# Attention and experts on one core: the first norm folded into the query weights, projections moved into the steps, token weights routed in two early parts

## The reference, cut to what matters

```python
def _layernorm(x, axis=-1, eps=1e-05):
    m = jnp.mean(x, axis=axis, keepdims=True)
    v = jnp.var(x, axis=axis, keepdims=True)
    return (x - m) / jnp.sqrt(v + eps)

# attention: q from the normed x, k and v from ctx
scores = jnp.einsum('bhqd,bhkd->bhqk', qh, kh) / scale        # scale = 8 ** -0.5
scores = jnp.where(mask, NEG_INF, scores)
attn = jax.nn.softmax(scores, axis=-1)
ctx = jnp.einsum('bhqk,bhkd->bhqd', attn, vh)                 # then @ Wo.T

# experts, on the flat normed tokens
logits = flat @ router_w.T
topk_scores, topk_idx = jax.lax.top_k(logits + router_bias, 2)
topk_scores = jax.nn.softmax(topk_scores, axis=-1)
combine = combine.at[jnp.arange(N)[:, None], topk_idx].add(topk_scores)
hidden = jax.nn.silu(gate_all) * up_all
out = jnp.einsum('nk,nkd->nd', combine, jnp.einsum('nke,ked->nkd', hidden, down_proj))
out = out + (jax.nn.silu(flat @ sh_gate.T) * (flat @ sh_up.T)) @ sh_down.T

x = x + attention(_layernorm(x), ctx, ctx, mask, ...)
x = x + experts(_layernorm(x), ...)
```

## Time and profile before

| | us |
|---|---|
| median of 3 runs | 194.75 (193.85 to 194.76) |
| the profiled execution, its own time | 194.68 |
| its span, first to last instruction | 192.9 |

### The profile page before, as it was taken

How to read it: one execution, slowest core, us unless ns; L and a number is a source line. 1 busy time by engine, 2 the same in 40 slices (tenths; PEclk the granted TensorE clock), 3 DMA queues, 4 the chain that set the end, 5 groups by cost and what they waited for, 6 DMA issues and landing times.

```text
span 192.9 us, 4173 instructions
## 1 busy us (share of the span) xinstructions
PE 179.3 (93%) x1351; PEld 131.8 (68%) x1351; DVE 168.8 (87%) x515; ACT 124.6 (65%) x280; POOL 92.1 (48%) x148
## 2 busy tenths in 40 slices
PE   7599599999999999999998799999999999999962
PEld 7497467566666666666666466778888888888841
DVE  6899999589999999989995799988899889988981
ACT  2168374777888888888885855466655665565641
POOL 5746992758988988888786690300000000000000
PEclk9969979999999999999999999999999999999997
DMA  5984910000000000000000174332363236324401
GB/s 135 286 249 92 352 40 0 5 0 0 3 2 5 0 3 0 3 0 2 5 0 3 57 198 139 110 110 82 128 180 115 72 126 171 120 82 126 120 0 54
DMA packets 13202, 15.33 MB, mean 79 GB/s; under 512 B 1665, under 2 KB 8193, under 8 KB 13057
## 3 DMA queue, kind: packets, MB, share of 16 engines
q1 hardware_dynamic: 12608, 14.57, 24.8%
q10 hardware_dynamic: 576, 0.55, 1.2%
HBM read 13.93 MB, written 1.18 MB: 78 GB/s over the span
## 4 chain that ended last, share of the span: by engine, by line
PE 61%; DVE 19%; ACT 5%; issue 5%; POOL 0%; DVEq 0%; POOLq 0%
PE bank L1013 26%; PE bank L964 12%; PE bank L945 5%; PE bank L954 5%; DVE hid L823 2%; PE bank L903 2%; ACT hid_hi L598 2%; PE bank L934 2%; DVE prob L759 2%; PE bank L924 2%; DVE smax L738 2%; DVE xn L649 2%; DVE hid_lo L815 2%; DVE cmix_sb L823 2%; PE bank L893 1%
## 5 line engine op out<-in xcount | busy, mean ns | idle before, releaser
L589 ACT ACTIVATE sig<-bank 128x512 f32<-128x512 f32 x36 | 21.5, 600 | 21.0 <-PE bank L1013 20.4
L964 PE MATMUL bank<-k_blk,q_blk 128*128 128x512 f32 x64 | 34.0, 615 | 0.0
L426 POOL TENSOR_TENSOR k_blk<-k_all,consts_sb 128x512 f32<-128x512 f32 x32 | 32.7, 1045 | 0.0
L1013 PE MATMUL bank<-xt_hi,w_hi 128*128 (+1 forms) x72 | 29.1, 405 | 0.0
L1013 PE MATMUL bank<-xt_lo,w_hi 128*128 (+1 forms) x72 | 28.4, 394 | 0.0
L1013 PE MATMUL bank<-xt_hi,w_lo 128*128 (+1 forms) x72 | 28.3, 393 | 0.0
L542 ACT COPY prob_t<-bank 128x512 f32<-128x512 f32 x32 | 18.8, 586 | 11.5 <-PE bank L945 11.5
L806 DVE TENSOR_TENSOR hid_u<-sig,bank 128x512 f32<-128x512 f32 x32 | 21.9, 684 | 4.2 <-PE bank L1013 2.5
L738 DVE TENSOR_REDUCE smax<-bank 128x8 f32<-128x512 f32 x32 | 21.9, 686 | 2.6 <-PE bank L964 2.6
L759 DVE TENSOR_TENSOR prob<-bank,smax 128x512 f32<-128x512 f32 x32 | 22.0, 687 | 0.6
L547 ACT ACTIVATE prob<-prob 128x512 f32<-128x512 f32 x32 | 20.8, 653 | 0.0
(11 more groups left out here) (116 smaller groups left out, 378.8 us busy)
## 6 DMA issues: line engine op xcount, KB each, us to landing
mix_all<-w_rows SPq DMA_DIRECT2D x64, 128.0 KB, 2.9
w_moe_sb<-w_moe SPq DMA_DIRECT2D x1, 1728.0 KB, 9.9
x_sb<-x SPq DMA_DIRECT2D x4, 256.0 KB, 7.6
ctxt_sb<-ctx_t SPq DMA_DIRECT2D x4, 256.0 KB, 5.9
ctx_sb<-ctx_nat SPq DMA_DIRECT2D x4, 256.0 KB, 5.1
out<-x_sb SPq DMA_DIRECT2D x3, 256.0 KB, 2.3
w_att_sb<-w_att ACTq DMA_DIRECT2D x1, 264.0 KB, 5.8
mrow<-mask_row ACTq DMA_DIRECT2D x1, 256.0 KB, 4.9
```

What stands on the lines that cost most here:

```text
L426: last = nc.gpsimd.tensor_tensor(k_blk[p][:, g, :, :], k_all[:, bass.ds(t, 1), g, :].broadcast_to([P, HG, S]), hmask_sb.rearrange("p (h o) ...
L589: nc.scalar.activation(sig[r][:, :], gate_ps[r][:, :], ACT.Silu).then_inc(s_sig, 1)
L964: nc.tensor.matmul(score_ps[g][:, :], q_blk[q][:, g, :, :].rearrange("p b s -> p (b s)"), k_blk[q][:, g, :, :].rearrange("p h s -> p (h s) ...
L1013: last = nc.tensor.matmul(out, w, moving, start=start and k == 0, stop=stop and k == 2)
```

## The change

- The first norm is folded. Queries are projected from the raw transposed x (a new input `x_t`) with the query weights multiplied by a centering matrix and by the score scale (`wqc_sb`); the division by the standard deviation becomes the scale of the exponential, one number per token (`rstd1`). Mean and variance of x are still taken (`moments`), now only for that scale.
- Keys: PE makes the mean of the valid keys of a sequence with one small product per tile (`key_means`, `w_mean`), DVE puts it at the masked columns of the transposed context (`mean_keys`, a predicated copy), PE projects the keys from there. The mean matrices, the masked context and the copies around them go.
- Only group 0 and the means and values of group 1 are projected ahead of step -1; group 1's queries and keys go into step -1, group 2 into step 0, group 3 into steps 1 and 2. Statistics of groups 1, 2 and 3 go to DVE's steps 0, 2 and 3, their `rstd1` to POOL's steps 1, 3 and 4.
- Loads: all of the context, the transposed context and x in both forms have buffers of their own; SP issues 21 loads in a row, the expert weights in four quarters.
- Routing: the token weights fall into three parts, tiles 0 to 3, 4 to 7 and 8 to 15 (`PARTS`). The first is routed in steps 6 to 9, the second in steps 10 to 13, the third as the second half before. Nothing of it is left in steps 14 and 15.
- The negated mean of the second norm moves from DVE into POOL's bias operation (now with two scalars). ACT's rounding of expert weights moves to the end of its step.

The core of the diff, by engine ("..." marks what is left out):

```diff
         # SP
+            sp.dma_start(consts_sb[:, :], consts).then_inc(s_const, 16)
+            load_group(0)      # ctxt_all, ctx_all, xt_all of group 0
+            load_group(1)
+            load_x(0)
+            load_group(2)
+            load_experts(0)
+            load_x(1)
+            load_group(3)
+            load_x(2)
+            load_experts(1)
+            load_x(3)
+            load_experts(2)
+            load_experts(3)
...
             store_rows(0)
             sp.wait_ge(s_w_rows, 16)
             for n in range(GROUPS * EPAIRS):
+                if n == SPREADS:
+                    store_rows(1)
+                if n == EPAIRS:
+                    sp.wait_ge(s_w_rows, 32)
                 if n == EPAIRS + SPREADS:
-                    store_rows(1)
-                    sp.wait_ge(s_w_rows, 32)
+                    store_rows(2)
+                    sp.wait_ge(s_w_rows, 48)
         # POOL
+            pool.wait_ge(s_const, 16)
+            pool.wait_ge(s_half, 3)
             rstd1_of(0)
-            ...
-            for g in range(GROUPS):
-                mix_of(g)
...
+            for t in range(2):
+                pool.wait_ge(s_q_sb, 1)
+                q_block(t, t, first=True)
+                pool.wait_ge(s_k_sb, 1)
+                k_blocks(t, t)
...
-                    nc.gpsimd.tensor_tensor(bias2[p][:, :], neg_mean2[p][:, :], rstd2[p][:, :], ALU.mult).then_inc(s_bias2, 1)
+                    nc.gpsimd.tensor_scalar(bias2[p][:, :], mv2[p][:, 0:1], rstd2[p][:, :], -1.0, ALU.mult,
+                                            ALU.mult).then_inc(s_bias2, 1)
...
+                if t == 1:
+                    rstd1_of(1)
+                if t in (3, 4):
+                    rstd1_of(t - 1)
         # ACT, in step
                 def exponentials(g):
                     act.wait_ge(s_sub[g], t + 2)
+                    if (t + 1) % GT == 0:
+                        act.wait_ge(s_rstd1, (t + 1) // GT + 1)
                     nc.scalar.activation(prob[q][:, g * GN:(g + 1) * GN], prob[q][:, g * GN:(g + 1) * GN], ACT.Exp,
-                                         scale=SCORE_SCALE).then_inc(s_exp[g], 1)
+                                         scale=rstd1[:, t + 1:t + 2]).then_inc(s_exp[g], 1)
...
                 if on(0):
                     transposed(1)
+                if t == 2:
+                    queries(3)
...
-                if isinstance(t, int) and t == TILES - 1:
-                    weights_to_sbuf(0)
+                if t == LEAD:
+                    keys(1)
+                if t == 0:
+                    queries(2)
+                    keys(2)
+                if t == 2:
+                    keys(3)
...
+                if t in (GT + 5, 2 * GT + 5):
+                    weights_to_sbuf(t // GT - 2)
         # DVE
+            def mean_keys(g):
+                dve.wait_ge(s_mask_row[min(g, 1)], 16)
+                dve.wait_ge(s_cm, g + 1)
+                dve.wait_ge(s_v, g + 1)
+                cols = slice(g * GN, (g + 1) * GN)
+                nc.vector.copy_predicated(
+                    ctxt_all[:, cols].rearrange("p (c s) -> p c s", s=S), mrow8[:, cols].rearrange("p (c s) -> p c s", s=S),
+                    cm_ps[g][:, 0:GT * BPT].rearrange("p (c o) -> p c o", o=1).broadcast_to([P, GT * BPT, S]))\
+                    .then_inc(s_pred, 1)
...
+            denominators(slice(0, GT))
+            mean_keys(0)
+            values_to_sbuf(0)
+            moments(0)
+            mean_keys(1)
+            values_to_sbuf(1)
...
         # DVE, at the end of step
-                if isinstance(t, int) and t == TILES - 4:
-                    top_two(0)
-                if isinstance(t, int) and t == TILES - 3:
-                    two_weights(0)
-                if isinstance(t, int) and t == TILES - 2:
-                    dve.wait_ge(s_w_top, 1)
-                    weigh_experts(nc.vector, 0)
-                    join_experts(dve, nc.vector, 0)
+                if t == 0:
+                    mean_keys(2)
+                    values_to_sbuf(2)
+                    moments(1)
+                if t == 1:
+                    mean_keys(3)
+                    values_to_sbuf(3)
+                if t == 2:
+                    denominators(slice(GT, TILES))
+                    moments(2)
+                if t == 3:
+                    moments(3)
+                if t in (GT + 2, 2 * GT + 2):
+                    top_two(t // GT - 1)
+                if t in (GT + 3, 2 * GT + 3):
+                    two_weights(t // GT - 1)
+                if t in (GT + 4, 2 * GT + 4):
+                    part = t // GT - 2
+                    dve.wait_ge(s_w_top, part + 1)
+                    weigh_experts(nc.vector, part)
+                    join_experts(dve, nc.vector, part)
         # PE
+            def key_means(g):
+                pe.wait_ge(s_ctx[g], 16)
+                ...
+                for i in range(GT):
+                    t = g * GT + i
+                    last = nc.tensor.matmul(cm_ps[g][:, i * BPT:(i + 1) * BPT], ctx_all[:, t, :],
+                                            w_mean[:, t * BPT:(t + 1) * BPT], start=True, stop=True)
+                last.then_inc(s_cm, 1)
...
             pe.wait_ge(s_half, 1)
             keep_busy(9)
+            for i in range(2):
+                nc.tensor.matmul(pvt_ps[:, i * P:(i + 1) * P], half_sb[:, :], half_sb[:, :], start=True, stop=True)
             pe.wait_ge(s_valid, 1)
             nc.tensor.matmul(count_ps[:, 0:BATCHES], half_sb[:, :], valid_key[:, :], start=True,
                              stop=True).then_inc(s_nvalid, 1)
-            keep_busy(5)
+            keep_busy(3)
+            pe.wait_ge(s_center, 1)
+            pe.wait_ge(s_wproj, 16)
+            nc.tensor.matmul(wqc_ps, center_sb[:, :], wq_sb, start=True, stop=True).then_inc(s_wqc, 1)
+            keep_busy(3)
+            key_means(0)
+            pe.wait_ge(s_wqc_sb, 1)
+            values_of(0)
+            queries(0)
+            keys(0)
+            key_means(1)
+            values_of(1)
         # PE, in step, in this order between the products that stay
+                if t == 0: key_means(2); values_of(2)          # ahead of scores(0)
+                if t == LEAD: queries(1)                       # from here ahead of scores(1)
+                if t == 1: key_means(3)
+                if t == 2: queries(3)
+                if t == LEAD: keys(1)                          # from here behind transposes(1)
+                if t == 1: values_of(3)
+                if t == 2: pe.wait_ge(s_v_sb, GROUPS)
+                if t == 0: queries(2)                          # from here ahead of values
+                if t == 2: keys(3)
+                if t == 0: keys(2)                             # at the end of the step
+                if t in (GT + 5, 2 * GT + 5): weights_as_rows(t // GT - 2)
-                if once and t == TILES - 1:
-                    weights_as_rows(0)
```

More of the change, by code:

```diff
@@ L598, in high_part, with weights_to_sbuf @@
                     nc.scalar.copy(hid_hi[k][:, cols], hid[k][:, cols]).then_inc(s_hid_hi, 1)
-            def weights_to_sbuf(half):
-                act.wait_ge(s_ct, half + 1)
-                nc.scalar.copy(comb_t[half][:, :], ct_ps[half]).then_inc(s_ct_sb, 1)
+            def weights_to_sbuf(part):
+                act.wait_ge(s_ct, part + 1)
+                nc.scalar.copy(comb_t[part][:, :], ct_ps[part]).then_inc(s_ct_sb, 1)
             def slot(g, m):
@@ new lines, in denominators @@
+            def denominators(tiles):
+                for e in range(2):
+                    rows = slice(e * S, (e + 1) * S)
+                    nc.vector.tensor_copy(
+                        v_all[rows, tiles, :, :, e, DK].rearrange("p t b j -> p (t b) j"),
+                        share_key[rows, tiles.start * BPT:tiles.stop * BPT].rearrange("p (c o) -> p c o", o=1)
+                        .broadcast_to([S, (tiles.stop - tiles.start) * BPT, PAIRS])).then_inc(s_vden, 1)
+            nc.vector.memset(v_all[:, 0:GT, :, :, :, :].rearrange("p t b j e d -> p (t b j e d)"), 0.0)\
@@ new lines, in queries, with keys @@
+            def queries(g):
+                pe.wait_ge(s_xt[g], 16)
+                if g > 1:
+                    pe.wait_ge(s_pred, g + 1)
+                elif g == 1:
+                    pe.wait_ge(s_q_sb, 1)
+                by_heads(wqc_sb, xt_all, g, q_ps).then_inc(s_q, 1)
+            def keys(g):
+                pe.wait_ge(s_pred, g + 1)
+                if g == GROUPS - 1:
+                    pe.wait_ge(s_q_sb, GROUPS)
+                elif g > 0:
+                    pe.wait_ge(s_k_sb, g)
+                by_heads(wk_sb, ctxt_all, g, k_ps[g]).then_inc(s_k, 1)
@@ L979, in step @@
                     transposes(0)
+                if t == LEAD:
+                    queries(1)
+                if t == 1:
+                    key_means(3)
+                if t == 2:
+                    queries(3)
```

(16 more changed lines are left out.)

426 lines of the change are left out of this document (179 added, 247 removed).

## The result

The changed kernel takes 198.8 us in the median of four runs (198.11 to 200.06), the kernel before 194.3 beside it: a ratio of 1.0244, interval 1.0198 to 1.0291. So it is slower, as forecast, but by 4.5 us and not by 1.3, and 198.8 lies 0.8 us above the upper end of the range. The profiled execution took 198.41 us, its span is 196.6 against 192.9; the 3.7 us between the spans are what the rows can account for.

The account below looks back on a forecast made before the run. VectorE bounds the opening, TensorE the steps from step 4 on. 194.68 us, +1.8 for a later step 6, +1.0 for routing, -1.45 at the end of the steps, gives 196.0 us; range 193.0 to 198.0.

Parts of the forecast that it names:

- the wait of step 0: Step 0: queries of group 2 wait for VectorE's predicated copy, which ends at 29.9; TensorE idles 2.0 us.
- the waits of step 2: Step 2: VectorE's late copy of group 3 delays the residual and group 3's keys; 1.5 us of waits.
- VectorE's delay at the attention transpose in step 4: VectorE ends step 3 0.8 us behind TensorE, which pays for it in step 4; step 5 starts at 56.2.
- POOL's late bias in step 5: Group 3's rstd at the end of POOL's step 4 makes step 5's bias 1.2 us late, 0.3 free: +0.9.
- Behind the steps: Step 15 and its tail: less VectorE work, no transposed weights or their copy; -1.45 us, carried to the experts.
- The costs without a row: Predicated copy 0.69 us (0.42 to 1.02), exp with scale per tile -0.1 to 0.2, POOL's two-scalar bias 0 to 0.4.
- part 2: The new start: first blocks, TensorE idle 4.3 us, step -1 5.2 us instead of 3.6, step 0 at 23.5.
- part 4: Routing in two parts: VectorE's blocked time beyond its slack in the steps costs +1.0 us (bounds 0 and 2.6).
- the slower rivals: Two cases, a second clock fall (chance 0.13) or blocking in the routing (chance 0.1), each giving 197.6 us.
- second fall: Clock falls again after step 0's 2.0 us of idle time, step 1 loses 1.6 us: 197.6; chance 0.13.
- the rival by blocking: All five operations of a routing part wait 0.5 us for POOL; two parts cost 2.6, not 1.0: 197.6; chance 0.1.
- the rival "faster": Clock stays up in step -1 (1.6), POOL's rstd hides (0.9), step 2's waits shrink (1.0): 192.5; chance 0.2.

Follow-up runs that it names:

- POOL's order mended: Changed kernel with POOL's rstd of group 0 moved behind the blocks of tiles 0 and 1; 193.26 us, 0.9955 against the kernel before.
- statistics early, rstd stays: Changed kernel with VectorE's statistics of groups 1 to 3 moved ahead of step -1 and behind it, POOL's rstd unmoved; 198.85 us, ratio 1.0222.
- the gap filled: Changed kernel with twenty unread 128x128 products in TensorE's idle stretch ahead of step -1; 197.29 us, 1.0140 against the kernel before.
- copy first: Changed kernel with the predicated copy of group 2 ahead of VectorE's row maximum in step 0; 196.97 us, 1.0153 against the kernel before.

## Why the prediction was wrong

**What held.** Slower; the first score at 18.74 (18.3 forecast), for the reason given, POOL's rstd ahead of the blocks; a fall of the clock behind the idle time; the wait of step 0; the waits of step 2; VectorE's delay at the attention transpose in step 4; POOL's late bias in step 5 (0.8 us, 0.9 forecast). From step 0 to step 5 no length is off by more than 0.2 us. Behind the steps -1.43 us was measured and -1.45 forecast; ScalarE's second table load stands 4.7 us behind the first gate (110.12 and 105.41) in place of 6.0. The costs without a row came out inside their bounds:

```profile
L526 ACT ACTIVATE prob<-prob,rstd 128x512 f32<-128x512 f32 x32 | 23.8, 743 | 1.9 <-DVE prob L779 1.9
...
L467 POOL TENSOR_SCALAR bias<-mv,rstd 128x1 f32<-128x1 f32 x16 | 4.2, 264 | 1.6
...
L644 DVE COPY_PREDICATED ctxt_all<-mrow,bank 128x512 f32<-128x512 uint8 x4 | 2.9, 729 | 2.6 <-PE bank L901 2.4
```

(groups of the changed kernel: count, busy us, mean ns, idle before): the predicated copy took 0.73 us where I took 0.69.

**First wrong step, the length of step -1 in part 2.** I took 3.6 us at full clock and charged 1.6 for the half clock. The runs show 4.1 at full clock (15.66 to 19.80 with POOL's order mended) and 6.6 in the changed kernel. 0.5 us is missing because I added the lengths of products that follow their like, 0.86 us for scores and 0.94 for queries and keys; set in turn they take 1.05 and 1.02. The other 0.9 us is the clock: I copied the fall that the rows of before showed behind 2.1 us of idle time, though I had put 4.3 us of it there. The clock was already at 0.50 when the first score began, and it held for all but the last 1.3 us of the step. The price at half clock was nearly the whole step's, not that of a piece. It is not the same in every execution: in the profile of "statistics early, rstd stays" TensorE idled 3.9 us there, the clock was up again by 22 us, and step -1 took 5.6 us:

```profile
20.00:21.00 1.00, 1.00 (x3) 0.30 (x4) 0.34 (x1) 0.00 (x0) 1.00 (x2) 0.50 1.01 347
22.00:23.00 1.00, 1.00 (x4) 0.30 (x2) 0.07 (x1) 0.80 (x2) 0.00 (x0) 1.00 0.76 302
```

So the fall cost 1.5 us in one profile and 2.5 in another. Together with a start 0.4 us later (x landed at 13.3 and not at 12.4, so its statistics began 0.5 late) step -1 makes +1.9 at step 0, of which the steps give back 0.4.

**Second wrong step, the routing in part 4.** The blocked time of a part was right: 2.0 us forecast, 2.05 in the chain of waits (0.53 in step 6, 0.42 in step 7, 1.10 in step 8; TensorE pays in the step behind). But I credited a part with slack of up to 0.4 us in each of its steps and then took off another 0.2 for lag that costs nothing. Steps 7, 8 and 9 of the changed kernel take 4.63, 4.53 and 5.34 us where 4.46 is the pace, 1.1 us a part and 2.2 for both, less 0.4 for the routing before: 1.8 (1.7 by the start of step 15), and I had +1.0. The difference of 2.05 blocked and 1.1 paid is a slack of 0.3 us in each of the three steps (an estimate from these rows); of lag only the 0.08 by which step 10 stays under the pace (4.38) came free.

These two make 2.2 of the 2.4 us between 196.0 and 198.41. Nearly all of the rest is that I took step 6 of before from the chain (59.92), where the timeline has 59.77.

**The range fell with them.** Its upper end, 198.0, left 0.4 us above either of the slower rivals taken alone (197.6). With the two terms at their measured size the sum is already 198.2, and the profiled execution, at 198.41, has no second fall (clock 1.00 from 25.36 to 63.18 us). Such a fall, which I gave a chance of 0.13 and counted from 196.0, comes on top of whatever else is wrong, at 1.6 us. The four runs of the changed kernel fit that: 198.1 and 198.4 us at a mean clock of 0.977 and 0.978, 199.2 and 200.1 at 0.970; which stretch lost the clock in the latter two is not recorded, so this part is argued, not shown.

Two smaller terms were off: POOL's spare time is 0.49 us a step by the rows that I named for 0.45, and the rival by blocking took all five operations of a part as held for 0.5 us, where the first of each row took 0.21.

None of the three savings of the rival "faster" came. It did not name the order of POOL's queue as a fourth, and the runs show that this alone decides: with the rstd of group 0 behind the blocks the wait goes and the clock stays up too, and step 6 starts at 57.6, before the 60.0 that I gave as the point of decision.

## What to carry to other kernels

Before an operation is put at the head of an in-order queue, list what stands behind it and who waits for that: here a power that only the first exponential needs held the first score product, and moving it behind the blocks turned 2.4% slower into 0.45% faster. An idle stretch of TensorE is to be priced with what runs behind it at the half clock, here 1.5 to 2.5 us on top of a wait of 3.9 to 4.6, and a filler or a changed order is worth a look wherever such a stretch is left. Small VectorE operations on SBUF were cheaper one to a step, started ahead of POOL's, than in a row.

## What was not expected of the hardware

- TensorE's clock fell behind idle stretches of 1.9 us in some executions and not in others: with 1.00 in the profiles of the changed kernel and of the one with POOL's order mended, with 0.50 for 3 us in the one with the gap filled and the one with statistics early where rstd stays. I found no row that tells the cases apart.
- An idle stretch in the opening counts too. TensorE idled 2.19 us up to 9.34 in the profile of before and 2.12 us up to 9.56 in that of "copy first", and the clock was 0.50 from 10 to 12 us in the one and from 11 to 14 in the other; the profile of the changed kernel has no such stretch and 1.00 there.
- The kernel before pays for it as well: over its runs beside these kernels the mean clock ranged from 0.973 to 1.000, and at 1.000 it took 193.3 to 194.3 us, its medians are 194.2 to 194.5.
- A VectorE operation of 128x64 on two SBUF inputs took 0.21 us where it began before POOL's operation and 0.48 to 0.54 where it began inside one.
